# The fifth and sixth block of a sorted feed-forward: second layer wholly in three-product parts, rows transposed by VectorE and DMA in place of TensorE

## What is computed

```
x = x + xattn(ctx_1024, layernorm(x))            # 16 heads of 64, keys from 128 + 128 rows
z = layernorm(x)
e = argmax(z @ centroids.T);  a = sigmoid(z @ centroids[e])
h = relu((layernorm(z) * ln_g[e] + ln_b[e]) @ w1[e].T + b1[e])     # 256 -> 1024
y = z + h @ w2[e].T + b2[e]                                          # 1024 -> 256
x = x + a * y + (1 - a) * z
```

## Time and profile before

| | |
|---|---|
| median of 3 runs | 1046.26 us (1046.17 to 1046.98) |
| the profiled execution | 1046.23 us |
| its span, first to last instruction | 1044.4 us |
| PE busy | 1033.8 us (99%) |
| DVE busy | 865.2 us (83%) |
| ACT busy | 711.7 us (68%) |
| POOL busy | 590.8 us (57%) |
| granted TensorE clock | 1.00 of full speed throughout (2.4 GHz) |

### The profile page before, as it was taken

One profiled execution on the slowest core, in us unless ns is written; L12 is line 12 of the kernel. 1 busy time (PEld: TensorE's weight loads), 2 busy tenths in 40 slices (PEclk: granted clock), 3 DMA queues, 4 the chain that ended last, 5 costly groups with the idle time before them and its releaser, 6 DMA issues.

```text
span 1044.4 us, 24949 instructions
## 1 busy us (share of the span) xinstructions
PE 1033.8 (99%) x8714; PEld 937.7 (90%) x8714; DVE 865.2 (83%) x2005; ACT 711.7 (68%) x1864; POOL 590.8 (57%) x709
## 2 busy tenths in 40 slices
PE   8999999999999999999999999999999999999997
PEld 7889898989888888888898989898988999999997
DVE  7877888889888888888888888888887796898884
ACT  6765757575756667676666575758556667998982
POOL 1754464636464554555554546464544466688885
PEclk9999999999999999999999999999999999999999
DMA  6666667575768575767676766757366878878750
GB/s 202 164 170 157 152 176 181 146 200 144 200 156 205 143 196 144 191 153 201 156 191 157 186 173 155 190 145 189 91 153 190 270 238 275 256 264 279 239 191 30
DMA packets 159666, 190.59 MB, mean 182 GB/s; under 512 B 17453, under 2 KB 149037, under 8 KB 154672
## 3 DMA queue, kind: packets, MB, share of 16 engines
q1 hardware_dynamic: 155088, 179.09, 63.0%
q0 software_dynamic: 3360, 8.53, 2.2%
q10 hardware_dynamic: 1088, 1.31, 0.4%
HBM read 65.72 MB, written 46.07 MB: 107 GB/s over the span
## 4 chain that ended last, share of the span: by engine, by line
PE 95%; DVE 2%; POOL 1%; DMA 1%; ACT 1%; issue 0%; ACTq 0%; POOLq 0%
PE psum L772 17%; PE psum L805 16%; PE psum L842 11%; PE psum L934 10%; PE psum L821 10%; PE psum L857 9%; PE psum L965 9%; PE psum L791 9%; PE psum L971 2%; PE psum L860 1%; DMA w_ring<-in_w_q 1%; PE psum L913 1%; PE psum L946 1%; DVE neg_max L1456 1%; PE psum L886 0%; DVE w_lo L1591 0%
## 5 line engine op out<-in xcount | busy, mean ns | idle before, releaser
L1873 POOL TENSOR_TENSOR prob<-prob,inv_sum 128x512 f32<-128x512 f32 x172 | 177.7, 1047 | 190.3 <-DVE inv_sum L1462 189.9
L1171 ACT ACTIVATE prob<-psum,neg_max 128x256 f32<-128x256 f32 x344 | 160.1, 478 | 39.1 <-DVE neg_max L1456 38.9
L1456 DVE TENSOR_REDUCE neg_max<-psum 128x2 f32<-128x512 f32 x256 | 161.8, 671 | 28.2 <-PE psum L821 28.2
L1468 DVE STREAM_TRANSPOSE prob<-prob 128x512 f32<-128x512 f32 x172 | 118.5, 698 | 12.3 <-POOL prob L1873 11.9
L1873 POOL TENSOR_TENSOR w_ring<-w_ring,inv_sum 128x512 f32<-128x512 f32 x76 | 78.1, 1040 | 76.3 <-DVE inv_sum L1462 76.0
L1178 ACT ACTIVATE head_out_hi<-psum 128x512 fp32r<-128x512 f32 x52 | 31.0, 596 | 105.6 <-PE psum L842 105.6
L1157 ACT ACTIVATE v_n<-psum 128x512 f32<-128x512 f32 x128 | 77.8, 608 | 26.7 <-PE psum L805 22.7
L1146 ACT ACTIVATE k_hi<-psum 128x512 fp32r<-128x512 f32 x128 | 77.0, 603 | 20.5 <-PE psum L772 19.5
L1507 DVE TENSOR_TENSOR k_lo<-psum,k_hi 128x512 fp32r<-128x512 f32 x128 | 85.6, 674 | 0.0
L772 PE MATMUL psum<-kv_t_hi,w_hi 128*128 128x512 f32 x252 | 85.0, 418 | 0.0
L1171 ACT ACTIVATE w_ring<-psum,neg_max 128x256 f32<-128x256 f32 x152 | 70.7, 477 | 15.8 <-DVE neg_max L1456 15.8
(11 more groups left out here) (220 smaller groups left out, 3012.3 us busy)
## 6 DMA issues: line engine op xcount, KB each, us to landing
sorted_rows<-filler SPq DMA_DIRECT2D x54, 660.0 KB
prob_t<-prob SPq DMA_DIRECT2D x172, 128.0 KB, 2.8
w_ring<-prob SPq DMA_DIRECT2D x172, 128.0 KB, 2.7
w<-in_experts SPq DMA_DIRECT2D x19, 1024.0 KB, 7.6
w_ring<-in_experts SPq DMA_DIRECT2D x18, 1024.0 KB, 6.1
prob_t<-w_ring SPq DMA_DIRECT2D x76, 128.0 KB, 2.8
w_ring<-w_ring SPq DMA_DIRECT2D x76, 128.0 KB, 2.7
w_ring<-normed SPq DMA_DIRECT2D x56, 128.0 KB, 3.1
```

Of the source, the lines that this page charges most:

```text
L1171: act.activation(prob_at(u, bb)[:, :, parity, i], scores_i, ACT.Exp, bias=neg_max[:, at, i:i + 1], accum_out=prob_sum[:, at, i:i + 1]).the ...
L1456: dve.tensor_reduce(neg_max[:, (4 * u + n) % 8, :], psum[:, n, :].rearrange("p (i j) -> p i j", i=2), AXIS_X, ALU.max, negate=True).then_i ...
L1468: dve.transpose(probs, probs).then_inc(s_quad, 1)
L1873: pool.tensor_tensor(probs, probs, inverse, ALU.mult).then_inc(s_soft, 1)
```

## The change

Two constants, `FIRST_MOVED = 4` and `FIRST_MORE = 4`, take the place of `n_early` (6) in all places that decide on the way of transposing and on the second layer. Slots 4 and 5 thus

- are transposed by VectorE (`transpose_rows`) and moved by SP's DMAs (`move_rows`), with the order on the engines changed for it, and TensorE's `row_transposes(4)` and `(5)` are gone;
- take all 8 chunks of the second layer in parts, with the relu in place in PSUM, 2 of 4 high halves of it on ACT, the whole of the second-layer weights split, and `layer_1(5)` waiting for `split_hidden(4)` bank by bank.

The core of the diff, in the order of the file: the banks' rotation and the two constants' uses, SP (`move_rows` and the loops), TensorE, ScalarE (`row_gain_bias`, `relu_parts`), VectorE.

```diff
-        order += [("ft", slot + 2) if slot + 2 < n_early else ("pass", slot, 0), ("fy", slot, 0), ("fy", slot, 1), ("pass", slot, 1)]
+        order += [("pass", slot, 0), ("fy", slot, 0), ("fy", slot, 1), ("pass", slot, 1)]
...
-                return psum[:, i, :] if s >= n_early else hid_raw[:, i, :]
+                return psum[:, i, :] if s >= FIRST_MORE else hid_raw[:, i, :]
...
-                return SPLIT if s >= n_early else SPLIT_EARLY
+                return SPLIT if s >= FIRST_MORE else SPLIT_EARLY
...
                 def move_rows(s):
-                    sp.wait_ge(f_xt, s - n_early + 1)
-                    if s == n_early:
+                    sp.wait_ge(f_xt, s - FIRST_MOVED + 1)
+                    if s == FIRST_MOVED:
                         wait_made(sp, ("wout", n_batches - 1))
                     else:
-                        sp.wait_ge(f_g, s - n_early)
+                        sp.wait_ge(f_g, s - FIRST_MOVED)
...
                     load_weights_1(s)
+                    if s == n_early - 1:
+                        move_rows(FIRST_MOVED)
                     load_weights_2(s - 1)
...
                 run(n_early + 1, (load_rows,))
+                for s in range(FIRST_MOVED + 1, n_early):
+                    move_rows(s)
                 run(n_early, (load_weights_1,))
...
-                        elif s > n_early and i < SPLIT // 2:
+                        elif s > FIRST_MORE and i < SPLIT // 2:
                             pe.wait_ge(f_hl, hidden_split(s - 2) + i + 1)
...
                 layer_1(3)
-                row_transposes(4)
                 layer_2_split(2)
                 for s in range(3, n_early):
                     layer_1(s + 1)
-                    if s + 2 < n_early:
-                        row_transposes(s + 2)
                     layer_2_split(s)
...
-                    if s > n_early:
+                    if s == FIRST_MOVED:
+                        wait_read(act, ("total",))
+                    elif s > FIRST_MOVED:
                         act.wait_ge(f_xd, 2 * (s - 1))
...
-                        if s >= n_early and 1 <= i <= 2:
+                        if s >= FIRST_MORE and 1 <= i <= 2:
                             high_hidden(s, i - 1)
...
                 split_xn(3)
+                transpose_rows(4)
                 finish(1)
...
                 split_hidden(3)
+                transpose_rows(5)
                 finish(2)
                 for s in range(3, n_early):
-                    if s + 2 == n_early:
-                        transpose_rows(s + 2)
                     low_weights_1(s + 2)
                     split_hidden(s + 1)
                     split_xn(s + 2)
-                    if s + 3 > n_early:
-                        transpose_rows(s + 3)
+                    transpose_rows(s + 3)
                     finish(s)
```

More of the change, by code:

```diff
@@ L35, with bank_order @@
 NW, NW2, NR, NBLOCK = 2, 3, 4, 7
+FIRST_MOVED = 4
+FIRST_MORE = 4
 FIRST_SPLIT = 1
 W_OUT_PIECES = 4
-def bank_order(n_pairs, last_of_early, n_early, n_slots):
+def bank_order(n_pairs, last_of_early, n_slots):
     n_steps = 4 * n_pairs
@@ L78, in bank_order @@
     order += [("ft", 1), ("fy", 0, 0), ("fy", 0, 1), ("rank", n_pairs - 2), ("pv", n_steps - 1), ("wout", n - 2), ("ft", 2), ("wout", n - 1)]
-    order += [("ft", 3), ("fy", 1, 0), ("fy", 1, 1), ("rank", n_pairs - 1), ("total",), ("ft", 4),
-              ("fy", 2, 0), ("fy", 2, 1)]
-    for slot in range(3, n_slots):
-        order += [("ft", slot + 2) if slot + 2 < n_early else ("pass", slot, 0), ("fy", slot, 0), ("fy", slot, 1), ("pass", slot, 1)]
+    order += [("ft", 3), ("fy", 1, 0), ("fy", 1, 1), ("rank", n_pairs - 1), ("total",)]
+    for slot in range(2, n_slots):
+        order += [("pass", slot, 0), ("fy", slot, 0), ("fy", slot, 1), ("pass", slot, 1)]
     return order
@@ L129, in build @@
     assert last_of_early % 2 == 1
-    assert 5 <= n_early <= n_sure - 2
-    order = bank_order(n_pairs, last_of_early, n_early, n_slots)
+    assert FIRST_MOVED + 2 <= n_early <= n_sure - 2
+    order = bank_order(n_pairs, last_of_early, n_slots)
     number = {item: i for i, item in enumerate(order)}
@@ L325, in xn_at @@
                     return c_in
-                item = ("ft", s) if s < n_early else ("pass", n_early, 1)
+                item = ("ft", s) if s < FIRST_MOVED else ("pass", n_early, 1)
                 return work_bank(number[item]).rearrange("p (c t) -> p c t", c=KC)
@@ L467, in wait_rows_moved @@
             def wait_rows_moved(eng, s):
-                eng.wait_ge(f_xm[s % 2], 4 * 16 * ((s - n_early) // 2 + 1))
+                eng.wait_ge(f_xm[s % 2], 4 * 16 * ((s - FIRST_MOVED) // 2 + 1))
             def wait_high(eng, g, side):
@@ L1213, in normalise_rows @@
                         wait_inputs_moved(act, n_pairs - 1)
-                    elif s < n_early + 2:
+                    elif s < FIRST_MOVED + 2:
                         wait_made(act, ("ft", s - 2))
@@ L1220, in normalise_rows @@
                         src, dst = row[:, 0:d_model], xhat[:, s % 2, i, :]
-                        if s >= n_early:
+                        if s >= FIRST_MOVED:
                             src = src.rearrange("p (c k j) -> p j c k", c=KC, j=4)
@@ L1229, in row_gain_bias @@
                     item = ("ft", s)
-                    if s < n_early:
+                    if s < FIRST_MOVED:
                         wait_made(act, item)
@@ L1278, in relu_parts @@
                         act.wait_ge(f_h, FC // 2 * (s - 1) + i + 1)
-                        if i < split // 2 and FIRST_SPLIT < s < n_early:
+                        if i < split // 2 and FIRST_SPLIT < s < FIRST_MORE:
                             act.wait_ge(f_hl, hidden_split(s - 1) - SPLIT_EARLY // 2 + i + 1)
@@ L1668, in split_xn @@
                 def split_xn(s):
-                    if s < n_early:
+                    if s < FIRST_MOVED:
                         wait_read(dve, ("ft", s))
                     else:
-                        dve.wait_ge(f_g, s - n_early + 1)
+                        dve.wait_ge(f_g, s - FIRST_MOVED + 1)
                     if s >= 3:
@@ L1690, in split_hidden @@
                             wait_made(dve, ("fy", s - 2, 1) if s > FIRST_SPLIT else ("pv", n_steps - 1))
-                        if s >= n_early and i < 2:
-                            dve.wait_ge(f_hh, 2 * (s - n_early) + i + 1)
+                        if s >= FIRST_MORE and i < 2:
+                            dve.wait_ge(f_hh, 2 * (s - FIRST_MORE) + i + 1)
                         else:
```

## The result

| | before | after |
|---|---|---|
| median (8 runs each) | 1046.59 us (1045.67 to 1049.31) | 1049.58 us (1047.7 to 1050.58) |
| median, measured a second time | 1046.19 us (25 runs) | 1048.97 us (10 runs) |
| the profiled execution, its span | 1046.23 us, 1044.4 us | 1050.27 us, 1048.5 us |
| PE busy | 1033.8 us | 1032.9 us |

After to before is 1.0027, 95% interval 1.0018 to 1.0037, and 1.0021 (1.0011 to 1.003) the second time. The change makes the kernel slower by 2.2 to 3 us, where I had forecast 1.9 us faster and ended the range at 1045.5.

The account below looks back on a forecast made before the run. TensorE was taken to bound the kernel: 2.02 us saved, less 0.1 for VectorE and about 0.05 for other margins, gives 1.87, so 1046.26 - 1.87 = 1044.4 us; range 1043.7 to 1045.5.

Parts of the forecast that it names:

- TensorE: TensorE's stream in slots 4 and 5: 0.88 us of transposes and 1.14 us of second layer go, 2.02 us together.
- VectorE before layer_1(5): VectorE's split rows for layer_1(5), ready at 869.1 or 869.8 against 869.58 wanted: 0.1 us lost, ends 0 and 0.25.
- Both of my cases: End of split_hidden(3) on VectorE: 859.2 if GpSimd's subtractions end as before, 859.9 if they are put off by 0.7.
- The move of slot 5's rows: SP's DMAs for slot 5: 5.3 to 7.35 us from issue to use; short one hidden, long one up to 0.9 lost.
- my signs of being wrong: TensorE idle over 0.5 us, ScalarE's x_cols wait over 2 us, ScalarE's w_ring wait, or late slots over 11.52 us.
- GpSimd: Low weights for slot 4 take 5.1 instead of 2.5 us, hidden before layer_2(4) with 1.9 us of cover or none.
- SP's queue: First-layer weights of slot 6, behind slot 5's move, land at 869.1 and may land by 871.7: hidden by 2.6 us.
- Slot 7: VectorE's rows for layer_1(7) ready at 892.2, wanted by TensorE at 892.6: holds by 0.4 us, bounds -0.3 and +0.7.
- each us costs a us: If GpSimd's cover before layer_2(4) goes, each microsecond late costs one microsecond.
- Slower: the weights of slot 6: Rival: slot 6's weights land past 871.7 behind slot 5's move, TensorE waits at layer_1(6); 1048.4 us or more; chance 0.05.
- Stalls at several slots: Rival: split_xn(4), (5), (7) or the moves come late, up to 1.8 us lost, 1044.6 to 1046.1; chance 0.18.

Follow-up runs that it names:

- the move ahead of the loads: Changed kernel with move_rows(6) issued ahead of the loads of w1(7) and w2(6) in SP's queue: 1047.21 us, ratio 1.0011.
- the other queue: Changed kernel with the move of slot 6's rows issued by ScalarE on its own DMA queue: 1048.97 us, ratio 1.0031.
- the second-layer half alone: Kernel before, with the second layer of slots 4 and 5 wholly in parts, their rows still transposed by TensorE: median 1044.85 us over both measurements.
- the moved half alone: Changed kernel with the second layer of slots 4 and 5 as it was before, rows still transposed by VectorE and moved: 1051.43 us, ratio 1.0056.
- the load ahead: Changed kernel with slot 6's first-layer weights loaded ahead of move_rows(5) in SP's queue: 1048.04 us, ratio 1.001.
- half the bytes: Changed kernel with w1(7) and w2(6) loaded by half, 0.5 MB each, the rest keeping older weights: 1046.13 us, ratio 1.0.

## Where the prediction was right and wrong

**TensorE, right.** 0.88 us of transposes and 1.14 us of second layer are gone, to the hundredth in the account above.

**VectorE before layer_1(5), right in its chain, wrong in its start.** From the end of split_hidden(3) I counted 9.9 us to the split rows; it is 861.42 to 871.21, 9.8. The start was not 859.2 or 859.9, but 861.42 (860.8 less this execution's 0.6). Both of my cases had GpSimd's subtractions at 854.0 or little later; they ran from 857.06 to 859.81, because ScalarE stood still for 3.70 us. The trace agrees with the rule of the Trainium skill that I had cited ("SBUF — State Buffer", Who interferes with whom): 1.28 and 1.67 us for 0.42 and 0.69, and 3.36 for 2.28. The margin that I counted at 0 to 0.25 us lost was 1.11 + 0.23. In the four executions with both halves of the change in which ScalarE ran on, this idle time was 0.13 us at most; in two of them, the move ahead of the loads and the other queue, VectorE's order was that of the kernel after. The forecast left no room for it, since nothing in the old trace showed it.

**The move of slot 5's rows, right.** 5.26 us from issue to use, the short end of my 5.3 to 7.35. One of my signs of being wrong showed here, a wait of ScalarE for x_cols of over 2 us before row_gain_bias(5): it was 2.60. It did not reach layer_1(5), since ScalarE was done at 868.39 and VectorE took the rows at 869.80, but it put off what ScalarE did next for slot 6.

**GpSimd, right.** The whole low half for slot 4 took 5.04 us and ended at 875.36, ahead of layer_2(4) at 877.30.

**SP's queue, the step that failed.** "Behind this move stands everything else of SP": I followed the one load directly behind, w1(6), found 2.6 us of cover for it, and it held: ScalarE didn't wait for w_ring. I asked whether each load would still be in time, and not what the loads, leaving together, would do to the next small transfer. I took 7.35 us as the upper end of a move because it was the longest in the old trace, "with 1 MB loads around it"; with four of them issued within 6 us shortly ahead of it, it takes 9.5 to 11.2, in the kernel after 9.64 and 10.24. That is the term mis-sized, by 2 to 4 us, for a move (slot 6's) which I named only as 1.6 us earlier than before. It was not earlier: 872.48 against 872.09. I had counted its start by VectorE alone, and ScalarE's normalising of these rows, behind slot 5's move and the whole high half, ended at 871.71.

**Slot 7, wrong by consequence.** 892.2 against 892.6 was counted without the late slot 6. Measured: 898.09 for the rows and 1.13 us of idle time.

**The price of standing still, missing.** I counted "each us costs a us". A stall of 1.1 to 2.3 us costs 0.22 us on top, as does one of 0.06 to 0.19, so that this part doesn't go by its length; one of 2.49 or more costs 1.7 to 2.6.

**The rivals.** "Slower: the weights of slot 6" had the right place in the program (SP's queue behind move_rows(5)), the right engine to wait (TensorE at layer_1(6)) and the wrong transfer. Its chance of 0.05 was so small because I excluded it by that one load's cover, and by the slots from 7 on, whose loads follow moves as closely. But there only two loads leave between one move and the next (878.04 and 882.74 ahead of 884.26, in the kernel before), and not four. Under "Stalls at several slots" I had priced the second-layer half alone at 1045.1 and argued for the moved half beside it; measured, the half alone is at 1044.85, and the moved half is the loss.

**What stays open.** ScalarE's standstill of 3.7 to 4.0 us at 849 to 853 shows in both executions of the kernel after, with the moved half alone, with the load ahead and with half the bytes. It shows for 2.9 us in the first execution of the second-layer half alone and not in the second, which is the same program, nor in the traces of the other kernels. So it belongs to the execution as well as to the program. Nothing that I ran tells what it waits for; that it carries the first idle time is read from the rows, not proved by taking it away.

## What to carry to other kernels

A wait that was put into a queue of loads cost twice here: it left the DMA engines idle, and then all held loads left together; look not for the load that comes late but for the next small transfer that has to share the engines with them, and price it by the bytes that still have to pass at its issue. Another queue did not help such a transfer while the engines were full; fewer bytes did. Loads moved behind one transfer stood ahead of the next. When a change has two halves that can be had apart, time them apart: one half here gave about 1 us, and the other took 5.

## What the runs showed of the chip

- A move of four transfers of 64 KB, SBUF to SBUF: 4.8 to 5.7 us from issue to use in the quietest cases, 6.1 to 8.8 us with loads of 1 MB closer ahead of it, 9.5 to 11.2 us with four issued within 6 us shortly ahead of it (370 to 414 GB/s from 874 to 882 us), and 10.8 on another queue.
- On the queue of the loads the move's first packet started 2.75 us after the issue with 0.85 MB ahead of it, and 6.11 us with 2.11 MB.
- After TensorE had stood still for 0.06 to 2.28 us, the next 48 products took 5.98 or 5.99 us in place of 5.76, at a granted clock of 1.00. After 2.49 to 3.01 us they took 7.42 to 7.48, at a granted clock of 0.77 or 0.78, and after 3.58 us they took 8.35, at 0.68. This is the stretch of the execution with slot 6's move on ScalarE's queue:

```profile
882.98:890.40 7.42, 7.42 (x50) 7.42 (x51) 5.42 (x6) 6.93 (x12) 6.90 (x5) 0.78 0.45 151
```

- One program's execution differed by 1 to 2 us ahead of the changed stretch (layer_1(4) starts between 856.3 and 858.5 us), which is as much as the change was to bring; the trace's account from a fixed instruction on was the sharper measure.
